# Earlier first transposes, loads of x from ScalarE's queue, and a last chunk computed in three passes, in a two-layer graph network on one Trainium2 core

## What is computed

```python
q, k, v = x @ Wq.T + bq, x @ Wk.T + bk, x @ Wv.T + bv
x = layernorm(x + softmax(q @ k.T / sqrt(512) + adj + adj) @ v)
h = relu(adj @ (x @ W1) + b1)
out = layernorm(x + adj @ (h @ W2) + b2)
```

## Time and profile before

| | us |
|---|---|
| median of 3 runs | 1943.66 |
| the profiled execution, its own time | 1943.4 |
| its span | 1941.6 |
| prologue until TensorE's first fp16 product | 32.1 |
| TensorE busy | 1905.0 |

### The profile page before, as it was taken

How to read it: one execution, slowest core, us unless ns; L and a number is a source line. 1 busy time by engine, 2 the same in 40 slices (tenths; PEclk the granted TensorE clock), 3 DMA queues, 4 the chain that set the end, 5 groups by cost and what they waited for, 6 DMA issues and landing times.

```text
span 1941.6 us, 25904 instructions
## 1 busy us (share of the span) xinstructions
PE 1905.0 (98%) x9008; PEld 877.2 (45%) x9008; DVE 1071.1 (55%) x2033; ACT 856.8 (44%) x1853; POOL 114.2 (6%) x206
## 2 busy tenths in 40 slices
PE   6899999999999999999999999999999999999997
PEld 3344444444444444444444444444444444444443
DVE  6776566666666666666666666666666620002223
ACT  3554455555555555555554555555555510101112
POOL 0000000000000000000000000000000000002334
PEclk9999999999999999999999999999999999999999
DMA  9565399999999999999999999999999999979995
GB/s 254 136 125 115 86 238 220 229 224 226 238 218 226 225 228 229 225 232 226 222 227 222 231 233 229 217 225 225 229 228 234 209 359 387 387 287 388 394 394 184
DMA packets 804804, 466.58 MB, mean 240 GB/s; under 512 B 649920, under 2 KB 657600, under 8 KB 804416
## 3 DMA queue, kind: packets, MB, share of 16 engines
q1 hardware_dynamic: 795168, 448.13, 92.1%
q10 hardware_dynamic: 9504, 16.79, 2.4%
HBM read 223.09 MB, written 92.01 MB: 162 GB/s over the span
## 4 chain that ended last, share of the span: by engine, by line
PE 94%; DVE 2%; DMA 2%; ACT 1%; SPq 1%; issue 1%; POOL 0%; ACTq 0%; POOLq 0%; DVEq 0%
PE bank L493 14%; PE bank L495 14%; PE bank L494 14%; PE bank L576 11%; PE bank L578 11%; PE bank L577 11%; PE bank L683 6%; PE bank L685 6%; PE bank L684 6%; PE bank L648 1%; DMA tsp<-tsp 1%; PE bank L500 1%; DMA adj_in<-in_L_gnn_Wk 0%; DVE x_sum L975 0%; SPq L422 0%
## 5 line engine op out<-in xcount | busy, mean ns | idle before, releaser
L792 ACT ACTIVATE tsp<-ring,sc 128x512 f16<-128x512 f32 x252 | 181.9, 722 | 623.1 <-DMA tsp<-tsp 622.8
L1133 DVE SCALAR_TENSOR_TENSOR ring<-bank,sc,adj_in 128x512 f32<-128x512 f32 x256 | 192.2, 751 | 381.2 <-PE bank L495 376.3
L576 PE MATMUL bank<-xv,tsp 128*128 128x512 f16 x1024 | 388.2, 379 | 6.1 <-DMA tsp<-tsp 5.6
L493 PE MATMUL bank<-xT,gT 128*128 128x512 f16 x1024 | 388.1, 379 | 0.0
L494 PE MATMUL bank<-xT,gT 128*128 128x512 f16 x1024 | 388.1, 379 | 0.0
L495 PE MATMUL bank<-xT,gT 128*128 128x512 f16 x1024 | 388.1, 379 | 0.0
L577 PE MATMUL bank<-xv,tsp 128*128 128x512 f16 x1024 | 388.1, 379 | 0.0
L578 PE MATMUL bank<-xv,tsp 128*128 128x512 f16 x1024 | 388.1, 379 | 0.0
L964 DVE SCALAR_TENSOR_TENSOR tsp<-adj_in,s_a,tsp 128x512 f16<-128x512 f32 x248 | 184.9, 746 | 64.1 <-ACT tsp L800 63.5
L964 DVE SCALAR_TENSOR_TENSOR tsp<-ring,sc,tsp 128x512 f16<-128x512 f32 x252 | 188.0, 746 | 6.4 <-ACT tsp L792 6.4
L784 ACT ACTIVATE ring<-ring,bias 128x512 f32<-128x512 f32 x256 | 180.9, 707 | 7.5 <-DVE bias L1150 7.5
(11 more groups left out here) (198 smaller groups left out, 2077.5 us busy)
## 6 DMA issues: line engine op xcount, KB each, us to landing
xv<-at_dram SPq DMA_DIRECT2D x66, 1024.0 KB, 11.1
adj_in<-in_adj SPq DMA_DIRECT2D x256, 256.0 KB, 3.3
at_dram<-tsp SPq DMA_DIRECT2D x248, 256.0 KB, 3.1
xT<-at_dram SPq DMA_DIRECT2D x21, 1024.0 KB, 14.0
adj_in<-at_dram SPq DMA_DIRECT2D x18, 1024.0 KB, 10.7
xv<-in_x SPq DMA_DIRECT2D x8, 1024.0 KB, 7.0
g_dram<-tsp SPq DMA_DIRECT2D x32, 256.0 KB, 4.0
gT<-g_dram SPq DMA_DIRECT2D x32, 256.0 KB, 3.6
```

The costliest lines, as they stand in the source:

```text
L493: pe.matmul(dst, ah, bh, start=(i == 0), stop=False)
L576: pe.matmul(dst, ah, vh, start=(kb == 0 and j == 0), stop=False)
L792: act.activation(p_split(e)[:, 0:BANK], p, ACT.Copy, scale=col[f"p_up{batch(TW * kb)}"]).then_inc(a_p, 1)
L1133: dve.scalar_tensor_tensor(t, s_bank[s % S_BANKS][:, :], col[f"k_l{batch(s // KB)}{batch(TW * (s % KB))}"], adj_in[:, s % AR, :], ALU.mult ...
```

## The change

**Prologue.** SyncE loads only groups 0 to 2 of x, the loads of W1 and b1 are moved behind tile 7's transpose. ScalarE issues the loads of groups 3 to 7: group 3 after a wait for the first transposed tile of x (`d_xt[0]`), group 4 behind the split of tile 4, groups 5 to 7 at the head of steps 0 to 2. ScalarE takes all sums but half of group 1's (two tiles on each engine). It splits tiles 0 to 3 ahead of the copy of the bias row, which waits for TensorE. GpSimd waits for ScalarE's sums itself and reduces all six columns of batch 1, and VectorE takes the maximum of the six. Tiles 8 and 9 are split one step earlier (step 5). On VectorE the maximum of Wv is put between the two bias products, the first block of Wv's low half ahead of its half sum, the maxima of M and of bv behind the first two low halves of x.

**Attention.** `load_gt` moves from the second to the fourth step of a row.

**End.** The last chunk is computed in three passes over its 8 units: tiles 0 and 1 of the chunk (256 columns, bank 1), tile 2 (128 columns, bank 4), tile 3 (128 columns, bank 5). `z_end` scales each pass's blocks, `END_AT` puts `o_rows` of tiles 24 to 30 between units, and only tile 31 stands behind the last matmul.

```diff
-ACT_SUMS = (0, 2, 3, 4, 6)
+SP_GROUPS = 3
+GT_AT = 3
+END = 2 * HALVES - NB
+PIECES = ((0, 2), (2, 1), (3, 1))
+PIECE_OF = [p for p, (_, count) in enumerate(PIECES) for _ in range(count)]
+END_AT = {(0, 3): 24, (0, 5): 25, (0, 7): 26, (1, 2): 27, (1, 6): 28, (2, 2): 29, (2, 6): 30}
...
@@ x_tiles_at
-        return {FIRST - 2: [FIRST, FIRST + 1, FIRST + 2], FIRST - 1: [FIRST + 3], FIRST: [FIRST + 4, FIRST + 5]}[t]
+        return {FIRST - 3: [FIRST, FIRST + 1], FIRST - 2: [FIRST + 2], FIRST - 1: [FIRST + 3],
+                FIRST: [FIRST + 4, FIRST + 5]}[t]
...
+        end_bank = [bank[1], bank[4], bank[5]]
...
@@ SyncE
-            sp.dma_start(w1_raw.rearrange(...), w1.rearrange(...)).then_inc(d_w1, 16)
-            sp.dma_start(b1_c[:, :], b1.rearrange("(p o) -> p o", o=1)).then_inc(d_b1, 16)
             load_x(X_FIRST)
...
             for t in range(XS + 1):
                 transpose_x(t)
-                if t in (1, 3):
-                    load_x(X_FIRST + 1 + t // 2)
             for t in range(NT):
                 for q in x_tiles_at(t):
                     transpose_x(q)
-                if t < NT // XG - X_FIRST - 3:
-                    load_x(X_FIRST + 3 + t)
                 if t == XG:
+                    sp.dma_start(w1_raw.rearrange(...), w1.rearrange(...)).then_inc(d_w1, 16)
+                    sp.dma_start(b1_c[:, :], b1.rearrange("(p o) -> p o", o=1)).then_inc(d_b1, 16)
...
-                if kb == 1 and 1 <= r < NT - 1:
+                if kb == GT_AT and 1 <= r < NT - 1:
                     sp.wait_ge(p_qk, KB * r)
                     load_gt(r + 1)
...
@@ TensorE, o_rows
-                if i == 0:
+                if n >= NT - TW:
+                    pe.wait_ge(a_z, k + 1 + PIECE_OF[i])
+                elif i == 0:
                     pe.wait_ge(a_z, k + 1)
...
-            for at in range(2 * HALVES):
+            for at in range(END):
...
-            for tile in outputs[-1]:
-                o_rows(tile)
+            pe.wait_ge(a_z, NC - 2)
+            for piece, (first, count) in enumerate(PIECES):
+                dst = end_bank[piece][:, 0:P * count].rearrange("p (i c) -> p i c", i=count)
+                for i in range(KB):
+                    load = holds[1, NC - 1, i]
+                    slot = loads[load][2]
+                    if piece == 0:
+                        pe.wait_ge(d_unit[slot], ...)
+                    for j in range(TW):
+                        wh, wl = h_hl[:, i, 0, j, :], h_hl[:, i, 1, j, :]
+                        rh, rl = (slots[slot][:, first:first + count, part * TW + j, :] for part in range(2))
+                        pe.matmul(dst, wh, rh, start=(i == 0 and j == 0), stop=False)
+                        pe.matmul(dst, wh, rl, start=False, stop=False)
+                        last = pe.matmul(dst, wl, rh, start=False, stop=(i == KB - 1 and j == TW - 1))
+                    if i == KB - 1:
+                        last.then_inc(p_end, 1)
+                    if (piece, i) in END_AT:
+                        o_rows(END_AT[piece, i])
+            o_rows(NT - 1)
...
@@ ScalarE
+            def load_x(i):
+                act.dma_start(xv[:, XG * i:XG * (i + 1), :], x_tiles[:, XG * i:XG * (i + 1), :]).then_inc(d_x[i], 16)
+
             def group_sum(i):
                 act.wait_ge(d_x[i], 16)
+                if i:
+                    act.wait_ge(a_xs, i)
+                tiles = xv[:, XG * i:XG * (i + 1), :] if i != 1 else xv[:, XG:XG + XG // 2, :]
+                column = i + (i > 1)
...
-            group_sum(ACT_SUMS[0])
+            group_sum(0)
             act.wait_ge(v_sc, 1)
-            for k in range(KD):
-                act.activation(wv_split[k][:, 0:D], wv_raw[:, k, :], ACT.Identity, scale=col["s_wv"]).then_inc(a_wv, 1)
+            wv_hi(0)
+            wv_hi(1)
+            group_sum(1)
+            wv_hi(2)
+            wv_hi(3)
+            for t in range(XS):
+                xt_hi(t)
+            group_sum(SP_GROUPS - 1)
             act.wait_ge(p_pre, KD + 3)
             act.activation(c_row, bank[7][:, :], ACT.Copy).then_inc(a_bias, 1)
-            for t in range(XS + 1):
-                xt_hi(t)
+            act.wait_ge(d_xt[0], 16)
+            load_x(SP_GROUPS)
+            xt_hi(XS)
+            load_x(SP_GROUPS + 1)
...
             for t in range(NT):
+                if SP_GROUPS + 2 + t < NT // XG:
+                    load_x(SP_GROUPS + 2 + t)
                 v_hi(t)
...
-                if 1 <= t <= len(ACT_SUMS) - 1:
-                    act.wait_ge(a_xs, t)
-                    group_sum(ACT_SUMS[t])
+                if SP_GROUPS + t < NT // XG:
+                    group_sum(SP_GROUPS + t)
...
+            def z_end(piece):
+                c = ORDER[1][NC - 1]
+                act.wait_ge(p_end, piece + 1)
+                if piece == 0:
+                    act.wait_ge(p_o, TW * (NC - Z_RING))
+                first, count = PIECES[piece]
+                for i in range(count):
+                    n = first + i
+                    last = act.activation(z_f[(NC - 1) % Z_RING][:, P * n:P * (n + 1)], end_bank[piece][:, P * i:P * (i + 1)],
+                                          ACT.Copy, scale=inv_z[:, TW * c + n:TW * c + n + 1])
+                last.then_inc(a_z, 1)
...
-            z_out(NC - 1)
...
+            finish(24)
+            finish(25)
+            z_end(0)
+            finish(26)
+            finish(27)
+            z_end(1)
+            finish(28)
+            finish(29)
+            z_end(2)
+            finish(30)
+            finish(31)
...
@@ VectorE
+                if b == 1:
+                    link(dve.tensor_reduce(col["mx_x1"], x_all[:, :], AX, ALU.max))
...
-                if t == 4:
-                    group_sum(5)
-                if t == 5:
-                    group_sum(7)
-                    dve.wait_ge(a_xs, len(ACT_SUMS))
-                    dve.tensor_reduce(col["st_x1"], x_sum[:, X_FIRST:NT // XG], AX, ALU.max).then_inc(v_st, 1)
...
@@ GpSimd
+            pool.wait_ge(a_xs, NT // XG)
+            pool.partition_all_reduce(x_all[:, :], x_sum[:, 3:NT // XG + 1], P, ALL_MAX).then_inc(g_ar, 1)
             pool.wait_ge(v_st, 5)
-            pool.partition_all_reduce(col["mx_x1"], col["st_x1"], P, ALL_MAX).then_inc(g_ar, 1)
-            pool.wait_ge(v_st, 6)
```

More of the change, by code:

```diff
@@ L149, in gnn_program @@
         b1_c = sb("b1_c", [P, 1], F32)
-        x_sum = sb("x_sum", [P, NT // XG], F32)
+        x_all = sb("x_all", [P, NT // XG - X_FIRST], F32)
+        x_sum = sb("x_sum", [P, NT // XG + 1], F32)
         gb_s = sb("gb_s", [P, 2, KD], F32)
@@ L267, in gnn_program @@
         d_out = [sem(f"d_out{i}") for i in range(O_RING)]
-        p_pre, p_v, p_g, p_qk, p_pv, p_y, p_adj, p_x1, p_unit, p_h, p_o = (
-            sem("p_" + s) for s in "pre v g qk pv y adj x1 unit h o".split())
+        p_pre, p_v, p_g, p_qk, p_pv, p_y, p_adj, p_x1, p_unit, p_h, p_o, p_end = (
+            sem("p_" + s) for s in "pre v g qk pv y adj x1 unit h o end".split())
         a_bias, a_xs, a_wv, a_m, a_w1, a_xt, a_v, a_gf, a_g, a_sum_s, a_exp, a_p, a_ah, a_x1, a_y, a_hs, a_h, a_z, a_o = (
@@ L690, in _ @@
                     o_rows(tile)
-            for tile in outputs[-1]:
-                o_rows(tile)
+            pe.wait_ge(a_z, NC - 2)
[5 more added lines that the diff above has]
+                    if piece == 0:
+                        pe.wait_ge(d_unit[slot], 16 * (sum(1 for l in loads[:load + 1] if l[2] == slot) + (slot < Y_DRAM // TW)))
+                    for j in range(TW):
[9 more added lines that the diff above has]
+            o_rows(NT - 1)
         @block.scalar
@@ L933, in _, with finish @@
                     store_output(tile)
-            z_out(NC - 1)
-            for tile in stored[-1]:
-                if tile in normed[-1]:
-                    o_normalise(tile)
+            def finish(tile):
+                o_normalise(tile)
                 store_output(tile)
+            for tile in range(NT - 2 * TW):
+                if any(tile in stored[at] for at in range(END, 2 * HALVES)):
+                    if any(tile in normed[at] for at in range(END, 2 * HALVES)):
+                        o_normalise(tile)
+                    store_output(tile)
+                if tile == NT - 2 * TW - 2:
+                    z_out(NC - 2)
+            finish(24)
[9 more added lines that the diff above has]
+            finish(31)
             for i in range(O_RING):
@@ L1060, in _ @@
             abs_max(col["st_gb"], gb_c[:, :]).then_inc(v_st, 1)
-            for t in range(2, XS):
-                xt_lo(t)
-            dve.wait_ge(d_bv, 16)
-            link(abs_max(col["mx_bv"], bv_row))
+            xt_lo(3)
             v_scale(0)
```

64 lines of the change are left out of this document (37 added, 27 removed).

## The result

The changed kernel took **1934.92 us** (median of 4 runs, 1933.74 to 1935.41), the kernel before, on the same chip, 1943.41 us (4 runs, 1942.90 to 1945.62). The ratio is 0.9954, 95% interval 0.9942 to 0.9966: faster by 8.5 us. The profiled execution took 1935.37 us with a span of 1933.6 us, 8.0 less than the 1941.6 of before.

A forecast was written before the change was run, and what follows sets the result against it. TensorE, busy for 98% of the span, was taken to bound the kernel, with gains only at the two ends: 1943.4 less 14.7 (prologue) less 3.2 (last chunk) gave 1925.5, or 1926 as median, range 1922 to 1934.

The forecast's parts named there:

- First transposed tile: Prologue: first product of x at 27.9 instead of 32.14, no slow clock behind it; gain 6.7 us.
- Tile 8: Prologue: TensorE reaches tile 8 at 60.7 instead of 75.36; gain 14.7 us, of which 6.7 were counted before.
- the cover of it: Prologue loads: group 7's load must land by 51.4; of a stop at tiles 2 to 4, about 1.5 us is absorbed.
- The prediction's own sign of being wrong: Prologue: the forecast is wrong if the granted clock falls between 28 and 60 us.
- Transposes held up by the loads of the other queue: Prologue rival: TensorE stops 3 to 4 us at tile 2, tile 8 near 66, time 1931; chance 0.22.
- Group 7 late anyway: Prologue rival: group 7's load ends where it did, tile 8 at 67, time 1932; chance 0.10.
- The clock never recovers: Prologue rival: repeated pauses of about 5 us, 7.8 each with slow clock, time 1949 at three; chance 0.03.
- Short matmuls: Last chunk rival: 128-column passes bound by 98 ns weight loads, 8.1 us lost, time 1934; chance 0.03.
- Last chunk: End: three passes leave less behind the last matmul, last statistics round 4.7 us after the old chunk end; gain 3.2 us.
- Moved without a cost: W1, b1 and `load_gt` moved later: counted as 0 us, bounds -0.5 and +1.

The follow-up runs named there:

- E9: E6 with ScalarE's four splits of x put back behind its wait for the bias row, as in the kernel before; 1931.62 us.
- E6: Changed kernel with loads of groups 3 to 7 on SyncE's queue, none ahead of a tile wanted before it; 1927.28 us.
- E3: Changed kernel, loads of x still on ScalarE's queue, but each issued only when the one before has landed; 1932.75 us.
- E7: Kernel before, with only the loads of groups 3 to 7 of x moved to ScalarE, behind the first transposed tile; 1955.96 us.
- E1: Kernel before with only the three-pass end of the last chunk added; 1941.53 us against 1943.14.
- E10: E6 with the load of g behind the first block of scores of a row again, not the third; 1927.39 us.
- E12: E6 with W1 and b1 loaded in their old place, ahead of group 2 of x; 1928.37 us.
- E8: E2 with W1 and b1 loaded in their old place and the load of g after a row's first block of scores; 1932.39 us.
- E2: Changed kernel with the loads of groups 3 to 7 of x back on SyncE's queue, in their old places between the transposes; 1929.22 us.
- E4: Changed kernel with all five loads of groups 3 to 7 issued together behind the first transposed tile; 1935.30 us.
- E5: Changed kernel with each load of x on ScalarE's queue cut into four, packets of 512 bytes instead of 2048; 1933.67 us.

## Why the prediction was wrong by half

**First transposed tile: right.** Transposes of Wv done at 24.64 (24.7 predicted), first product at 28.04 (27.9), idle 1.73 (1.1), no slow clock there. In E9 undoing it cost 4.3 us, in a kernel whose tile 8 also waits for its own chain; the 6.7 of the term were not measured by themselves.

**Tile 8: wrong, 71.0 and not 60.7, and it is the whole error.** 14.7 us were counted for the prologue, 4.3 came. The failed step is not the chain of sums and scales. It is the cover of it: "four loads and the transposes share the DMA engines", for which the sum had no term at all, with "about 1.5 us" of any stop taken in by the wait for tile 8, and the sentence against the rival, "at most two loads are queued at once". Three were, from 31.34 on. I had read group 7's issue as about 42 (39.95 it was), but groups 5 and 6 were issued at 31.34 and 34.08, since an issue on ScalarE's queue stands behind nothing but the waits ahead of it in the program, and each load took 6.0 to 10.7 us to land in this traffic. Tile 2's first packet moved only when the first of them was nearly through, 4.7 us after the issue. The prediction's own sign of being wrong, a granted clock that falls between 28 and 60, came true. With the order mended (E6) tile 8 is reached at 62.5 and the last sum ends at 55.4 where I had 60.7 and 53.4. So the schedule itself was short by 2 us, and the other 8.5 (71.0 less 62.5) are what the loads did to the transposes, at nothing in the sum.

**The rival had the mechanism, not its size.** "Transposes held up by the loads of the other queue" gave a stop of 3 to 4 us, one fall of the clock, tile 8 at 66 and 1931. Measured: 6.46 and 1.96 us, two falls, 71.0, 1934.9. The mis-sized term was "4 to 5 us more for tiles 2 and 4": tile 2 had 8.2 more (11.4 against the 3.2 of the earlier trace rows) and tile 3 13. I took them from a load beside a full queue, where both sides are plain loads. That the transposes' packets are eight times smaller was in the trace of before. The Trainium skill ("DMA: Bandwidth & Descriptors", Queues, rings and completion order) says that each DMA engine goes round the queues a packet at a time. By that rule I called the rival "mild", since a transpose "would always get its share". The counts of packets agree with the rule once tile 2 moves (565 and 562, 670 and 672). My reading of it was wrong: a share by packet is one ninth of the bytes here. And the trace shows no share at all for the tile from 28.9 to 33.1 us, where the loads moved 465 packets and the transposes none; the rule as I used it doesn't account for that.

**Group 7 late anyway:** not in the changed kernel, whose sum 7 ended at 59.1 without waiting for its load, well ahead of the late TensorE. It is the rival that held in E3.

**The clock never recovers:** not here, but E7 is this case, with stops of 5.34, 5.96 and 6.08 us, a clock of 0.50 behind each, and 13.3 us slower than before. I had asked for transposes "over 8 us apart"; in E7 tiles 3 and 4 were.

**Short matmuls:** no. Those of 128 columns are 0.056 apart (eleven starts from 1912.29 to 1912.85), as the earlier trace rows had it; the 98 ns of the earlier trace rows bound nothing.

**Last chunk: right.** 2.8 us for 3.2 in the changed kernel and in E1. The old end of the chunk would be at 1922.3 (1898.11 + 24.15), and the last round of statistics began 5.1 behind it for 4.7 predicted.

**Moved without a cost:** right for each move alone (E10, E12); E8 leaves some 3 us of both together, if they are real, unexplained. The 0.8 us between tile 8 and the last chunk were outside my sum; TensorE's waits for `tsp` fell by as much, from 5.6 to 4.8 us, and which move did that isn't shown.

## What to carry to other kernels

Before a stream of loads is moved to a second queue, count the packets of what stays behind: two full queues of the same DMA engines shared by packet here (562 to 565, 1209 to 1267), so that the transposes' packets of 250 bytes lost to the loads' 2 KB by the ratio of their sizes. Look also at what is issued just ahead in the other queue: here a tile waited for most of it. What is wanted first and what is wanted later belong in one queue, in the order of their due times; one queue in that order gave 7.6 us over the changed kernel, of which 5.7 came with the one queue (E2) and some 2 with the order (E6). And a stop counts with the clock behind it: where one of 5 us is taken away, look whether the new order brings another.

## What the runs showed of the hardware

- A transposed tile of 256 KB takes 3.2 us to land alone. Beside loads of 2 KB packets on the other queue it takes 6.4 (1 MB outstanding), 11.4 (2 to 3 MB) and 10.5 (5 MB); beside packets of 512 bytes 4.9. I had expected it to grow with the backlog; it levels off. What stays alike is the number of load packets that pass the tile, 1404 to 1561 in the changed kernel, E4, E5 and E7, be they 2 KB or 512 bytes.
- With a load issued ahead of it on the other queue, the tile's first packet moved 4.7 us after its issue in the changed kernel and 4.5 in E3 and E4; behind a first part of 256 KB it was 2.0 (E5), and with nothing ahead 1.2 (E6).
- An engine's queue can hold up its own issue: SyncE's instruction for tile 3 took 5.64 us, and those of tiles 4 and 5 11.23 together, against 1.23 to 1.3 each in quiet. What stands behind such a transpose in SyncE's program is issued late too. ScalarE's issues can be held up as well: five loads took it 5.84 us in E4, against 0.37 to 0.49 for one in the changed kernel.
- The clock can fall behind a stop of 1.96 us (0.55 in 46 to 48 us) when it had fallen shortly before, while one of 1.19 in the kernel before left it at full rate. In E6 stops of 1.16 and 1.52 left it alone, and in E2 one of 2.35 took it to 0.53. The length of the stop alone doesn't settle it: in E5 one of 2.48 left the clock at 1.00, and one of 2.04, some 5 us later, was followed by 0.50.
